# A two-layer graph network on one core: the table of TensorE's gather in two float32r terms, a second of its tiles in every third supertile, and another order of the start

## The reference

```
h = max(layernorm(x), 0)
x = x + segment_sum(h[src] * edge_weight, dst)          # layer one
h = max(layernorm(x), 0)
hid = relu(edge_attr_32 @ W1 + b1); w = hid @ W2 + b2   # 4 x 8 x 8 weights for each edge
m0, m1 = products of h[src], edge_attr_4 and w          # a scalar and a vector part
x = x + segment_sum([m0, m1], dst) + h @ si             # layer two
```

## Time and profile before

| | us |
|---|---|
| median of 3 runs | 6810.92 |
| lowest and highest | 6810.56 to 6811.79 |
| the profiled execution | 6811.97 |
| its span, first to last instruction | 6810.2 |
| busy: TensorE, VectorE, GpSimd, ScalarE | 6352.5, 4936.7, 5083.4, 2996.4 |
| layer one's gathers | 49.7 to 3196.7 |
| layer two's gathers | 3246.2 to 6766.4 |

### The profile page before, as it was taken

How to read it: one execution, slowest core, us unless ns; L and a number is a source line. 1 busy time by engine, 2 the same in 40 slices (tenths; PEclk the granted TensorE clock), 3 DMA queues, 4 the chain that set the end, 5 groups by cost and what they waited for, 6 DMA issues and landing times.

```text
span 6810.2 us, 173887 instructions
## 1 busy us (share of the span) xinstructions
PE 6352.5 (93%) x50435; PEld 3306.6 (49%) x50435; DVE 4936.7 (72%) x11425; ACT 2996.4 (44%) x13299; POOL 5083.4 (75%) x5424
## 2 busy tenths in 40 slices
PE   5999999999999999997899999999999999999998
PEld 2544444444444444444455555555555555555554
DVE  6655555555555555555788888888888888888887
ACT  1222222222222222223666665666666566666665
POOL 5777777777777777777777777777777777777776
PEclk9999999999999999998999999999999999999998
DMA  3111111111111111111211111111111111111111
GB/s 94 28 26 26 27 26 27 26 26 27 26 26 27 26 26 27 26 27 22 47 36 36 35 36 35 36 35 35 35 36 35 35 36 36 35 35 36 35 35 33
DMA packets 353046, 224.61 MB, mean 33 GB/s; under 512 B 114285, under 2 KB 349373, under 8 KB 352509
## 3 DMA queue, kind: packets, MB, share of 16 engines
q0 software_dynamic: 170080, 87.42, 9.6%
q1 hardware_dynamic: 182390, 133.02, 7.1%
q10 hardware_dynamic: 548, 3.84, 0.2%
HBM read 218.75 MB, written 5.12 MB: 33 GB/s over the span
## 4 chain that ended last, share of the span: by engine, by line
POOL 64%; issue 23%; PE 10%; POOLq 1%; DVE 1%; DMA 0%; ACT 0%; SPq 0%; DVEq 0%; ACTq 0%
POOL z L421 64%; PE w_ps L660 3%; PE hp_ps L788 2%; PE w_ps L741 1%; PE sc_ps L757 1%; PE w_ps L745 1%; PE w_ps L730 1%; POOLq L418 0%; POOLq L419 0%; POOLq L417 0%; PE w_ps L670 0%; PE w_ps L737 0%; POOLq L234 0%; PE w_ps L701 0%; PE sc_ps L760 0%
## 5 line engine op out<-in xcount | busy, mean ns | idle before, releaser
L421 POOL DMA_INDIRECT z<-h_table,idx x5315 | 5028.9, 946 | 1657.9 <-issue 1610.1
L660 PE MATMUL w_ps<-stage,prod 128*128 128x448 bf16 x13125 | 2595.0, 354 | 86.0 <-DVE prod L980 78.9
L660 PEld LDWEIGHTS w_ps<-stage,prod 128*128 128x128 bf16 x13125 | 1234.0, 98 | 1203.3 <-issue 92.4
L510 ACT ACTIVATE z<-z,squares 128x32 f32<-128x32 f32 x3125 | 733.2, 309 | 2331.1 <-DMA z<-h_table,idx 2241.2
L788 PE MATMUL hp_ps<-stage,squares 128*128 128x448 bf16 x6510 | 1340.8, 354 | 9.8 <-DVE stage L1198 9.8
L972 DVE TENSOR_TENSOR acc<-acc,w_ps 32x32 f32 x1250 | 213.0, 170 | 1289.9 <-PE w_ps L670 1281.0
L788 PEld LDWEIGHTS hp_ps<-stage,squares 128*128 128x128 bf16 x6510 | 586.0, 98 | 598.5 <-issue 107.4
L611 ACT ACTIVATE near<-iota_sb,rel_sb 128x32 f32<-128x32 f32 x3125 | 725.1, 312 | 0.0
L568 ACT ACTIVATE coef<-z,ft_sh_sb 128x32 f32<-128x32 f32 x3125 | 721.1, 306 | 0.0
L1122 DVE TENSOR_TENSOR prod<-w_ps,coef 128x960 f32<-128x960 f32 x625 | 719.5, 1151 | 1.7
L980 DVE TENSOR_TENSOR prod<-sc_ps,feat 128x896 bf16<-128x896 f32 x625 | 682.3, 1092 | 51.4 <-issue 43.7
(11 more groups left out here) (95 smaller groups left out, 5585.2 us busy)
## 6 DMA issues: line engine op xcount, KB each, us to landing
z<-h_table,idx POOLq DMA_INDIRECT x5315
feat<-key_table SPq DMA_DIRECT2D x311, 192.0 KB
ft_sh_sb<-in_ft_sh SPq DMA_DIRECT2D x625, 90.0 KB
h_table<-big SPq DMA_DIRECT2D x10, 312.5 KB
x_sb<-in_x SPq DMA_DIRECT2D x5, 312.5 KB
prod<-in_dst_flat ACTq DMA_DIRECT2D x1, 1562.5 KB
rel_sb<-in_dst_t ACTq DMA_DIRECT2D x1, 1562.5 KB, 9.1
out<-x_sb SPq DMA_DIRECT2D x5, 312.5 KB
```

Source lines behind the costliest of these rows:

```text
L421: pool.indirect_dma_start(z[:, r, u, :], None, rows, bass.IndirectOffsetOnAxis(ap=idx[:, r, u:u + 1], axis=0)).then_inc(z_in[r], 16)
L510: last = nc.scalar.activation(z[:, r, u, :], z[:, r, u, :], ACT.Copy, scale=ew_all[:, bass.ds(n * G + u, 1)])
L660: mm = pe.matmul(fold_ps[:, k, 0:NC * D], pick[k][:, blk, :], parts[:, t, :, blk, :], start=(blk == 0 and t == 0), stop=(blk == GB - 1 and ...
```

## The change

1. The table is kept as two terms of type float32r instead of three of bfloat16: `parts` has a buffer of its own, ScalarE writes the first term, one subtraction gives the second. The selections are float32r too, in four buffers of their own. Both layers use them: 14 matmuls a tile instead of 21.
2. In layer one, TensorE gathers a second tile in every third supertile (r = 2 and 5), and GpSimd three instead of four. Selections, PSUM banks and semaphores count tiles now: four slots for the four tiles of three supertiles. Each batch of keys comes in two loads.
3. `acc` is cleared by ScalarE, behind the square roots of the start and not by GpSimd.
4. `rel_sb` is loaded by SP behind the table, not by ScalarE. The first half of the table is loaded before the wait for the padding, and its split waits for that half alone.
5. VectorE splits the table first; the positions within the window (`window_slots`) come in turn 3 of layer one, the widest span in turn 5.
6. Buffers: `stage`, the bias and some constants lie in `prod`.

The diff, cut to its core:

```diff
-            pool.memset(acc[:], 0.0).then_inc(cleared, 1)
...
-            supertiles(pool, R0, gathers(R0, h0_dram, idx0_ready, z0_in, sum0_ready, lambda r, s: GT))
+            supertiles(pool, R0, gathers(R0, h0_dram, idx0_ready, z0_in, sum0_ready, lambda r, s: gathered_by_pool(r)))
...
+    def gathered_by_pool(r):
+        return GT - 1 if r % PERIOD == PERIOD - 1 else GT
+    def first_pick(b, r):
+        return b * (R0 // PERIOD * SLOTS) + r + r // PERIOD
+    def picks_of(r):
+        return G - gathered_by_pool(r)
...
+        parts_flat = sb("parts", [P, 2, KD], F32R)
+        pick = sb("pick", [P, SLOTS, GB, P], F32R)
+        pick_banks = (0, 1, 2, PEG + 2)
...
+                half = KD // D // 2
+                cuts = [0, half // 2, half, (half + whole) // 2, whole]
                 def load_piece(q):
-                    load_blocks(h0_dram, cuts[q], cuts[q + 1]).then_inc(table_in, 16)
+                    load_blocks(h0_dram, cuts[q], cuts[q + 1]).then_inc(table_in[q // 2], 16)
                 sp.wait_ge(h_out, 16 * CH)
+                load_piece(0)
+                load_piece(1)
                 sp.wait_ge(table_padded, 1)
...
                 if s == 0:
                     load_tables()
+                    sp.dma_start(rel_sb[:].bitcast(I32), dst_t).then_inc(dstt_in, 16)
                     share_bases()
...
-                    sp.wait_ge(pick_ready, n - R0 + BATCH)
+                    sp.wait_ge(pick_ready, first_pick(b - 1, r) + SLOTS)
...
+                if count == BATCH:
+                    extra = R0 + r // PERIOD
+                    sp.dma_start(key[:, extra:extra + 1, :], key_dram[...]).then_inc(keys_in[r // BATCH], 16)
...
-            nc.scalar.dma_start(rel_sb[:].bitcast(I32), dst_t).then_inc(dstt_in, 16)
+            act.wait_ge(ones_set, 3)
+            nc.scalar.activation(acc[:], one_sb[0:D].to_broadcast([D, AW]), ACT.Copy, scale=0.0).then_inc(cleared, 1)
...
-            act.wait_ge(table_in, 16 * (4 + (N % P > 0)))
-            for t in range(2):
-                for h, half in enumerate(table_halves):
-                    if t > 0:
-                        act.wait_ge(split_dve, h + 1)
-                    nc.scalar.activation(flat_parts[:, t, half], table[:, half], ACT.Copy).then_inc(split_act, 1)
+            for h, half in enumerate(table_halves):
+                act.wait_ge(table_in[h], 16 * (2 + h * (N % P > 0)))
+                nc.scalar.activation(parts_flat[:, 0, half], table[:, half], ACT.Copy).then_inc(split_act, 1)
...
+                    for e in range(picks_of(r)):
+                        i, k = first_pick(b, r) + e, (first_pick(0, r) + e) % SLOTS
+                        pe.wait_ge(pick_ready, i + 1)
+                        if s is None or s >= PERIOD:
+                            pe.wait_ge(selected, i - SLOTS + 1)
+                        for blk in range(GB):
+                            for t in range(2):
+                                mm = pe.matmul(fold_ps[:, pick_banks[k], 0:NC * D], pick[:, k, blk, :], parts[:, t, :, blk, :],
+                                               start=(blk == 0 and t == 0), stop=(blk == GB - 1 and t == 1))
+                        mm.then_inc(picked, 1)
...
+            def split_table(parts_cut, rest_cut):
                 for h, half in enumerate(table_halves):
+                    dve.wait_ge(parts_cut, h + 1)
+                    nc.vector.tensor_tensor(parts_flat[:, 1, half], table[:, half], parts_flat[:, 0, half].bitcast(F32),
+                                            ALU.subtract).then_inc(rest_cut, 1)
...
+            def make_picks(b, r, s):
+                dve.wait_ge(keys_in[r // BATCH], b * 32 + (32 if whole else 16))
+                for e in range(picks_of(r)):
+                    i, k = first_pick(b, r) + e, (first_pick(0, r) + e) % SLOTS
+                    if s is None or s >= PERIOD:
+                        dve.wait_ge(picked, i - SLOTS + 1)
+                    nc.vector.tensor_tensor(pick[:, k], rows_ps..., key[:, R0 + r // PERIOD if e else r]..., ALU.is_equal
+                                            ).then_inc(pick_ready, 1)
...
                 if s is None or s < S:
-                    make_pick(n, b, r, s)
+                    make_picks(b, r, s)
                 if s is None or 3 <= s <= S + 2:
                     bv, v = before(b, r, R0, 3)
+                    if s == 3:
+                        window_slots()
                     one_hots(n - 3, v, iota_ps)
-                    select_group(n - 3, bv, v)
+                    for e in range(picks_of(v)):
+                        select_group(bv, v, e)
```

More of the change, by code:

```diff
@@ L21 @@
 PEG = 3
-BATCH = 3
+PERIOD = 3
+SLOTS = PERIOD + 1
+BATCH = PERIOD
 GB = 7
@@ L28 @@
 F32 = mybir.dt.float32
+F32R = mybir.dt.float32r
 BF16 = mybir.dt.bfloat16
@@ L339, in load_keys @@
                              ).then_inc(keys_in[r // BATCH], 16)
+                if count == BATCH:
+                    extra = R0 + r // PERIOD
+                    sp.dma_start(key[:, extra:extra + 1, :],
+                                 key_dram[bass.ds(b * (R0 // PERIOD) + (S + r // PERIOD), 1)].rearrange("s a e -> a s e")
+                                 .to_broadcast([P, 1, P])).then_inc(keys_in[r // BATCH], 16)
             def load0(b, r, s):
@@ L649, in sum0 @@
                 n = b * R0 + r
-                k = r % PEG
                 if s == 0:
-                    pe.wait_ge(split_dve, 4)
+                    pe.wait_ge(split_dve, 2)
                 if s is None or s < S:
-                    pe.wait_ge(pick_ready, n + 1)
-                    if s is None or s >= PEG:
-                        pe.wait_ge(selected, n - PEG + 1)
-                    for blk in range(GB):
-                        for t in range(3):
-                            mm = pe.matmul(fold_ps[:, k, 0:NC * D], pick[k][:, blk, :], parts[:, t, :, blk, :],
-                                           start=(blk == 0 and t == 0), stop=(blk == GB - 1 and t == 2))
-                    mm.then_inc(picked, 1)
+                    for e in range(picks_of(r)):
[8 more added lines that the diff above has]
+                        mm.then_inc(picked, 1)
                 if s is None or s >= 4:
@@ L786, in half_gather @@
                     for blk in range(GB // 2, GB) if on_pe(r) else range(GB // 2):
-                        for p in range(3):
-                            mm = pe.matmul(picked_ps, pick1[t][:, blk, :], parts[:, p, :, blk, :],
-                                           start=(blk == 0 and p == 0), stop=(blk == GB - 1 and p == 2))
+                        for p in range(2):
+                            mm = pe.matmul(picked_ps, pick[:, t, blk, :], parts[:, p, :, blk, :],
+                                           start=(blk == 0 and p == 0), stop=(blk == GB - 1 and p == 1))
                     if on_pe(r):
@@ L1193, in reduce @@
                         sum_groups1(b, r)
-                if s in (2, 3):
-                    for h, half in enumerate(table_halves):
-                        dve.wait_ge(split1_act, (s - 2) * 2 + h + 1)
-                        rest = flat_parts[:, 2, half] if s == 3 else table[:, half]
-                        nc.vector.tensor_tensor(rest, table[:, half], flat_parts[:, s - 2, half], ALU.subtract
-                                                ).then_inc(split1_dve, 1)
+                if s == 2:
+                    split_table(split1_act, split1_dve)
                 if s is None or s < S:
```

148 lines of the change are left out of this document (71 added, 77 removed).

## The result

The changed kernel takes **6608.54 us** (median of 4 runs, 6605.06 to 6609.11) against 6811.07 for the kernel before in the same comparison: a ratio of 0.97, with a 95% interval of 0.9689 to 0.9712. The forecast was 6537 us. The time lies inside the range (6510 to 6650), but outside the forecast's own (6510 to 6560): what happened in layer one is rival 3, to which I gave 0.07, and layer two became longer besides.

The account below looks back on a forecast made before the run. GpSimd's gathers were taken to bound the kernel, not the 98% busy TensorE. Fewer gathers 259.5, start 5 and first wait 10 sum to 274.5 us, giving 6537 us; own range 6510 to 6560, with some of rival 3 6510 to 6650.

Parts of the forecast that it names:

- rival 3: Layer one: matmul pace slightly over the edge (0.212 to 0.243 us), or VectorE's extra work makes the loop late; chance 0.07.
- GpSimd bounds, one gather is 1.247 us, 208 of them are 259.5 us: Layer one: GpSimd stays the bound, so moving 208 gathers to TensorE saves 259.5 us.
- The pace p = 0.194: TensorE: a float32r matmul of 448 columns takes the bfloat16 time, 0.194 us, as one product per element suffices.
- 42p + 4.83: Layer one's TensorE and VectorE loop per three supertiles, p the matmul pace: 13.0 us, under GpSimd's 13.72.
- the edge: Layer one: p = 0.212 us, where the loop reaches GpSimd's 13.72; above it every nanosecond costs 8.8 us.
- rival 1: Table products on TensorE: float32r weight loads not hidden, 88 ns more a matmul, p = 0.282, total 7237 us; chance 0.07.
- rival 2: TensorE, both layers: float32r streams as float32 does, p = 0.41, total about 9170 us; chance 0.05.
- rival 4: Layer one: gathers do not set the pace after all, time within 0.2% of before; chance 0.01.
- VectorE's selection at nothing more: VectorE: selections of four-byte elements still take 1092 ns; slower by up to 0.2 us, the loop still fits.
- The start, -5: Start: first gather comes at about 44.6 us instead of 49.7, with rel_sb's load out of the stores' stretch: -5 us.
- GpSimd's first wait for TensorE, 7 us: Start of layer one: TensorE starts at 66.2, so GpSimd waits 7 us instead of 16.96: -10 us.
- Layer two unchanged: Layer two: gathers unchanged, TensorE falls to about 9.6 us per pair but GpSimd still needs 11.23, so nothing counted.

Follow-up runs that it names:

- run 2: Changed kernel without the second tile: in layer one TensorE gathers one tile in every supertile, GpSimd four; 6812.33 us.
- run 11: Changed kernel with run 1's order in layer one, run 9's order and PSUM operand in layer two, and ScalarE's index copies after all square roots; 6539.28 us.
- run 12: Run 1's kernel with five of a tile's seven blocks in layer one multiplied over 224 columns instead of 448, every load as before; 6551.55 us.
- run 1: Changed kernel; in layer one's two-tile turns VectorE makes the second selection and select only after the first group select; 6556.06 us.
- run 10: Changed kernel with layer two's VectorE product issued ahead of the window reductions, its operand t011 left in SBUF; 6582.68 us.
- run 4: Kernel before with only two of its three bfloat16 terms used in layer two, 14 matmuls a tile instead of 21; 6825.38 us.
- run 3: Changed kernel with 21 float32r products a tile in layer two again, the second term taken twice; 6657.38 us.
- run 9: Changed kernel with layer two's VectorE product issued ahead of the window reductions, its operand t011 kept in PSUM; 6593.31 us.

## Why the prediction was right and wrong, point by point

- **GpSimd bounds, one gather is 1.247 us, 208 of them are 259.5 us.** Right, and shown from two sides: run 2 without them gains nothing, run 11 has 802 gathers in both windows and the predicted time. In the changed kernel itself GpSimd did not stay the bound, so 44 us of it went elsewhere.
- **The pace p = 0.194.** This is the step that failed. The reason given for it (one product per element, no second instruction) held, 11662 instructions for 11662 products, but that only excludes 0.82 us; it does not make the two paces equal. It measured 0.213, 10% more. The form of the loop, 42p + 4.83, was right: with p = 0.213 it gives 13.78, and the rest to the measured 13.91 is VectorE's path, 4.10 and not 3.97. By the prediction's own price above the edge, (13.91 - 13.72) x 208 = 40 us are lost, 44 were. Of the 40, 12 are p above the edge and 27 the longer path, which would have cost nothing had p been 0.194. Had I put p's uncertainty beside the edge (9% between 0.194 and 0.212), rival 3 would have been worth far more than 0.07.
- **The weight load.** The doubt behind rival 1 was right and its price wrong: the load's row did double (188 ns), and is hidden for the most part (run 12). The Trainium skill's rule ("TensorE: Matmul & The Clock Gate", Weight-path perf modes), fast weight load for types other than FP32 alone, agrees with the 188 ns if float32r counts as FP32. The price that rival 1 put on such a load, p = 0.282, did not come.
- **float32r streams as float32** (rival 2, 9170 us) and **gathers don't bind** (rival 4): refuted, the one by 0.213 a product, the other by run 11.
- **VectorE's selection at nothing more**: right, 1088 ns. But the rival had also named "VectorE's extra work makes the same loop late", and its order is what decided, as run 1 shows.
- **The start, -5.** The amount was right (4 in the other runs; 2.1 in the profile, where an index load came late), the parts were not: the clear's move, for which ScalarE's time was weighed at 0, is worth 0.6 at most. The transfers are left for the rest, which is not shown.
- **GpSimd's first wait for TensorE, 7 us.** It was 15.0, in the timeline of the changed kernel:

```profile
70.64 19.95 PE L683 MATMUL w_ps<-parts,pick 128*128 128x448 f32 x84 [70.64 <-DVE pick L997]
```

  TensorE starts at 70.64, not 66.2, as the keys arrive at 69.4: their four loads are issued behind the bases' (64.83 to 66.25), and I had let them come with the bases. That is 4.4 us; the 84 matmuls take 19.95 and not 18.3 at the slower pace, 1.7; GpSimd arrives 0.9 earlier, and the last microsecond is the window sum and the release behind the matmuls.
- **Layer two unchanged.** Wrong by 17 us. The sentence "TensorE loses 7 of 21 matmuls per pair (to about 9.6 us), but GpSimd still needs 11.23" costed relief at nothing, with no bound above it, though the earlier trace rows showed gathers of 3.80 us beside VectorE. In its place stand gathers held by one VectorE product that begins with them: the excess of the long ones, 23 us against 6, is the 17 us, and with the product elsewhere (run 10) it is gone. What sets the phase between the two is open.
- **The hand-over unchanged.** Wrong by 7.0 us, and it is the same late loop (run 1: 49.4).

Not tried: the two-tile turn with three bfloat16 terms (84 products a turn instead of 56). At 0.194 it would need 16.3 us + 1.3, more than 13.72, so the cut to two terms is what makes room for the second tile; that is worked out, not run.

## What to carry to other kernels

Compare the period by count of each engine and each closed loop, not its busy share: TensorE was 98% busy without binding, and relief on it alone was worth 0 (run 2) or -14 us (run 4). When a change leaves two engines within a few per cent of each other, write down the loop between them, put the uncertainty of each price beside the distance to the edge, and look at the order of work within the turn: the same instructions in another order were worth 52 us here. An engine that is relieved moves in phase, and the engine that binds can be held by operations that it seldom met before (10 gathers in layer two, then 147).

## What the runs showed of the hardware that was not expected

- A float32r matmul of 128 weights and 448 columns is one instruction at 0.213 us in a run of them (0.194 for bfloat16), with a load row of 188 ns (98) that overlaps the stream.
- A gather with which a VectorE product of 120 elements on SBUF operands begins (0.12 us before to 0.05 after) takes up to 1.13 us and not 0.94 in the changed kernel, and up to 1.32 if a second such product follows at once. It does so where the product starts while VectorE's operation ahead of it still runs (765 of 768 gathers). Where the product waited for the one ahead, as in runs 9 and 10, 2 of 62 were long, whether both operands lay in SBUF or one in PSUM.
- A gather held this way shows no wait: in run 3 all of the 52 us more lie in the durations of the gathers.
- TensorE's mean granted clock was 0.95 and 0.94 in the windows of runs 2 and 12, where it was busy for 755 and 775 of 1000 us. It is a mean of the two levels: in run 12, where TensorE had waited 1.96 us before 1499.54, the clock is 0.50 (1.2 GHz) from 1500 to 1502 us and 1.00 (2.4 GHz) from 1506 to 1508.2, and 28 products take 5.63 us in the one turn's first part beside 14 in 2.20 in the second. It cost nothing, as the gathers set the pace (802 and 801).
